# A Mamba block with an FP4 feed-forward layer on one core: where the C rows come from, and which VectorE operands lie in PSUM

## The reference

```
x = x + mamba(layernorm(x))
x = x + ffn(layernorm(x))
```

```
delta = softplus(dt_proj(dt_r) + dt_b)
s = s * exp(delta * A) + (delta * u) * B_t        # 128 channels x 16 states per head
y_t = sum over the 16 states of s * C_t
out = ((y + u * Dskip) * silu(z)) @ out_proj.T
```

## Time and profile before

| | |
|---|---|
| median of 3 runs | 6185.75 us (6184.68 to 6187.2) |
| span of the profiled execution | 6181.4 us |
| VectorE busy | 6057.9 us, 98% |
| GpSimd busy | 4848.8 us, 78% |
| TensorE busy | 4735.1 us, 77% |
| ScalarE busy | 4198.7 us, 68% |
| mean of the transfers | 10 GB/s |

### The profile page before, as it was taken

The page is one execution under the profiler, slowest core; times in us unless marked ns, Lnnn a source line. Parts: engine busy times, 40 slices in busy tenths (PEclk is TensorE's granted clock), DMA queues, the critical chain, the costliest instruction groups (busy, mean ns, idle before and its releaser), DMA issues.

```text
span 6181.4 us, 90775 instructions
## 1 busy us (share of the span) xinstructions
PE 4735.1 (77%) x14623; PEld 2333.3 (38%) x14892; DVE 6057.9 (98%) x8285; ACT 4198.7 (68%) x7312; POOL 4848.8 (78%) x4113
## 2 busy tenths in 40 slices
PE   4777777777777777777777777777777777777778
PEld 1233333333333333333333333333333333333334
DVE  7999999999999999999999999999999999999998
ACT  5766766676666667666676676666766766676663
POOL 6888777777787778777777787777777877787875
PEclk9999999999999999999999999999999999999999
DMA  1000000000000000000000000000000000000000
GB/s 43 5 8 9 9 9 11 9 9 9 12 8 9 9 12 9 9 9 11 9 9 9 12 9 9 9 11 9 9 9 11 9 9 9 12 9 9 9 6 13
DMA packets 59893, 62.59 MB, mean 10 GB/s; under 512 B 7014, under 2 KB 58342, under 8 KB 59110
## 3 DMA queue, kind: packets, MB, share of 16 engines
q1 hardware_dynamic: 57536, 53.68, 2.8%
q10 hardware_dynamic: 1702, 2.16, 0.1%
HBM read 39.04 MB, written 16.78 MB: 9 GB/s over the span
## 4 chain that ended last, share of the span: by engine, by line
DVE 45%; issue 26%; PE 21%; DVEq 4%; ACT 3%; POOL 1%; another core or an unknown queue 0%; DMA 0%; ACTq 0%; POOLq 0%
DVE state L824 14%; DVE db L814 8%; DVE acc L763 8%; PE ybank L892 6%; PE pbank L901 3%; DVEq L97 3%; PE db L879 3%; PE bank_b L947 2%; DVE v L647 2%; DVE spw L708 2%; PE bank_a L1017 2%; ACT decay L408 1%; DVE hh L758 1%; PE cbank L870 1%; PE bank_a L980 1%
## 5 line engine op out<-in xcount | busy, mean ns | idle before, releaser
L558 POOL TENSOR_TENSOR prod<-state,cs 128x512 f32<-128x512 f32 x2048 | 2777.2, 1356 | 1068.2 <-DVE state L824 1025.6
L395 ACT ACTIVATE cs<-cbank 128x512 f32<-128x512 f32 x2048 | 1217.0, 594 | 1184.3 <-PE cbank L870 993.4
L408 ACT ACTIVATE decay<-delta,aneg 128x512 f32<-128x512 f32 x2048 | 1455.1, 716 | 607.2 <-DVE state L824 599.4
L879 PE MATMUL db<-pieces,sel 128*128 128x512 bf16 x2031 | 807.5, 398 | 1345.7 <-DVE state L824 1309.8
L892 PE MATMUL ybank<-prod,ident 128*128 128x512 f32 x3072 | 1626.7, 619 | 2.7 <-POOL prod L562 2.6
L814 DVE TENSOR_TENSOR db<-db,du 128x512 f32<-128x512 f32 x2048 | 1394.4, 681 | 46.8 <-PE db L879 28.3
L824 DVE TENSOR_TENSOR_SCAN state<-decay,carry,db 128x512 f32<-128x512 f32 x1024 | 1286.7, 1257 | 0.0
L824 DVE TENSOR_TENSOR_SCAN state<-decay,db 128x512 f32<-128x512 f32 x1024 | 1229.3, 1200 | 0.0
L879 PEld LDWEIGHTS db<-pieces,sel 128*128 128x128 bf16 x2048 | 199.5, 97 | 2245.9 <-DVE state L824 2157.8
L562 POOL TENSOR_TENSOR prod<-prod 128x512 f32<-128x512 f32 x512 | 690.7, 1349 | 40.1
L870 PE MATMUL cbank<-pieces,sel 128*128 128x512 bf16 x1797 | 699.2, 389 | 14.9 <-ACT cs L395 13.9
(11 more groups left out here) (125 smaller groups left out, 7017.3 us busy)
## 6 DMA issues: line engine op xcount, KB each, us to landing
xin<-in_hidden SPq DMA_DIRECT2D x128, 128.0 KB, 2.0
xres<-in_hidden SPq DMA_DIRECT2D x128, 128.0 KB, 2.1
out_x<-ot SPq DMA_DIRECT2D x128, 128.0 KB, 1.9
win<-in_win_t SPq DMA_DIRECT2D x1, 1024.0 KB, 10.3
sel<-in_sel SPq DMA_DIRECT2D x1, 1024.0 KB, 14.9
state<-in_w_gate ACTq DMA_DIRECT2D x1, 704.0 KB
state<-in_w_up ACTq DMA_DIRECT2D x1, 704.0 KB
yg<-in_w_down ACTq DMA_DIRECT2D x1, 704.0 KB, 18.3
```

What stands on the lines that cost most here:

```text
L395: act.activation(cs[:, gc.k % RING, :], cbank[:, :], ACT.Copy).then_inc(c_copied, 1)
L408: act.activation(decay[:, g.k % RING, :], delta[:, gu % 2, :], ACT.Exp, scale=aneg[:, gu % HEADS, gn:gn + 1]).then_inc(decayed, 1)
L558: pool.tensor_tensor(prod[:, gn % RING, :], state[:, gn, :], cs[:, gn % RING, :], ALU.mult).then_inc(weighted, 1)
L879: pe.matmul(db[DB_BANK[g.k % TRIP]][:, :], sel[:, gn, :], pieces[:, gu % 2, :], start=True, stop=True).then_inc(b_spread, 1)
```

## The change

**C rows.** The matmul into `cbank`, the copy to `cs` and the upper half of the selection matrix go. ScalarE still makes `xdbl` in SBUF; SyncE now writes its 16 C rows to a DRAM buffer `c_rows` (32 KB for a unit), and reads them back two rows at a time, each pair as one transfer that repeats 4 KB on all 128 partitions (512 KB), into a ring of 4 buffers. A pair is asked for when the pair four places earlier has been weighted. GpSimd multiplies two states in one instruction of 1024 columns (`weigh`), and adds the two halves for the pairs 0, 2, 4 and 6 (`ADDED`), so the number of identity matmuls stays at 12 for a unit.

**Operands in PSUM.** The bank set free is `bank_c`. `z` is projected into it, while `x` stays in `pbank` and the convolution is carried out in place there (ScalarE makes tap 3, VectorE taps 0 to 2, with the shifted `x` from SBUF). `uu` reads `pbank`, the softplus correction reads `1 + e` from `bank_c`, and `yt` is written straight to `yg`.

**FP4 rounding.** ScalarE writes |x| times 2^22 to `bank_c`. VectorE reads the upper 16 bits of each word as BF16 and makes `x + max(that, ROUNDER)` and then the same with minus: two instructions for `v2`, and two for each half (352 columns) of `hh`.

Several slots move with it; `yt` goes from step 2 to step 3.

```diff
-PAIRED = (1, 6, 12, 14)
+PAIRS = NST // 2
+C_RING = 4
+P_RING = 4
+ADDED = (0, 2, 4, 6)
...
+            def spread_c(b, u, p):
+                slot = p % C_RING
+                free = held(sp, free_reg, u.val(PAIRS, p + 1 - C_RING))
+                if p == 0:
+                    rows_in = held(sp, rows_reg, u.val(16, 16))
+                    wait(sp, c_written, rows_in)
+                wait(sp, weighted, free)
+                rows = c_rows[u.mod(2), 2 * p:2 * p + 2, :].rearrange("n c -> (n c)")
+                sp.dma_start(cs[:, slot, :, :].rearrange("p n c -> p (n c)"),
+                             rows.unsqueeze(0).broadcast_to([P, 2 * CH])).then_inc(c_landed[slot], 16)
...
+                if n % 2:
+                    p = (n + 5) // 2
+                    w = u + p // PAIRS
+                    if w.within(UNITS):
+                        spread_c(b, w, p % PAIRS)
...
-                    act.activation(cs[:, gc.k % RING, :], cbank[:, :], ACT.Copy).then_inc(c_copied, 1)
+                if t := due("post", 48):
...
+                    act.activation(bank_c[:, 0:HALF], hv[t.mod(2)][:, 0:HALF], ACT.Abs, scale=POWER).then_inc(h_abs, 1)
...
+            def weigh(w, p):
+                c, r = p % C_RING, p % P_RING
+                wait(pool, scanned, w.val(NST, 2 * p + 2))
+                wait(pool, c_landed[c], w.val(16 * PAIRS // C_RING, 16 * (p // C_RING + 1)))
+                wait(pool, summed, w.val(PAIRS, p + 1 - P_RING))
+                pool.tensor_tensor(prod[:, r, :, :], state[:, 2 * p:2 * p + 2, :], cs[:, c, :, :],
+                                   ALU.mult).then_inc(weighted, 1)
...
-                dve.scalar_tensor_tensor(acc[:, :], xpad[:, h, k:k + CH], cw[:, h, k:k + 1], acc[:, :],
+                dve.scalar_tensor_tensor(pbank[:, :], x[:, k:k + CH], cw[:, h, k:k + 1], pbank[:, :],
...
+            def magnitude(n):
+                return bank_c[:, 0:n].bitcast(BF16).rearrange("p (n h) -> p n h", h=2)[:, :, 1]
+            def step_up(n, x):
+                return dve.scalar_tensor_tensor(hw[:, 0:n], magnitude(n), ROUNDER, x, ALU.max, ALU.add)
+            def step_down(n, x):
+                return dve.scalar_tensor_tensor(x, magnitude(n), ROUNDER, hw[:, 0:n], ALU.max, ALU.subtract)
...
-                    wait(pe, c_copied, g.val())
-                    pe.matmul(cbank[:, :], sel[:, NST + gn, :], pieces[:, gu % 2, :],
-                              start=True, stop=True).then_inc(c_spread, 1)
```

More of the change, by code:

```diff
@@ L102, in fresh, with held @@
     return b if isinstance(b, int) else eng.snap(b, min_val=1, max_val=BATCH - 2)
+def held(eng, reg, value):
+    if isinstance(value, int):
+        return value
+    eng.reg_mov(reg, value)
+    return reg
 def build(nc, hidden, win_t, conv_w, conv_b, xw, dtw, dt_b, a_log, dskip, wo_t, w_gate, w_up, w_down,
@@ L190, in build @@
         db = [bank(f"db{i}") for i in range(3)]
-        cbank = bank("cbank")
         ybank = bank("ybank")
         pbank = bank("pbank")
+        bank_c = bank("bank_c")
         bank_a = bank("bank_a")
@@ L361, in unit @@
-                t_o = Ix(b, j - 8, PER)
-                if t_o.within(TILES):
-                    wait(sp, o_done, t_o.val(plus=1))
-                    sp.dma_start(out_tiles[t_o.val()], ot[:, t_o.mod(2), :]).then_inc(ot_free[t_o.mod(2)], 16)
+                for n in range(NST):
+                    step(b, j, n)
             trips(sp, unit, constants)
@@ L462, in step @@
-                    act.activation(acc[:, :], xpad[:, h, 0:CH], ACT.Identity, bias=cb[:, h:h + 1],
-                                   scale=cw[:, h, 0:1]).then_inc(conv_op, 1)
+                    wait(act, x_mm, v.val(plus=1))
+                    wait(act, conv_op, v.val(TAPS))
+                    if v.mod(PER) < HEADS:
+                        act.activation(xearly[:, TAPS - 1:], pbank[:, :], ACT.Copy).then_inc(x_evac, 1)
+                        act.activation(halo[:, h, :], pbank[:, CH - TAPS + 1:], ACT.Copy).then_inc(x_evac, 1)
+                    else:
+                        wait(act, x_evac, v.val(2, -6))
+                        act.activation(xlate[:, 0:TAPS - 1], halo[:, h, :], ACT.Copy).then_inc(x_evac, 1)
+                        act.activation(xlate[:, TAPS - 1:], pbank[:, :], ACT.Copy).then_inc(x_evac, 1)
@@ L862, in step @@
                     spread_b(b, g)
-                for back in YSUM_BACK[n]:
-                    gy = Ix(b, j * NST + n - back, TRIP)
-                    if gy.within(STEPS) and gy.k % NST + 1 not in PAIRED:
-                        sum_up(b, gy)
+                if n % 2 == 0:
+                    w = u + (n - 4) // NST
+                    if w.within(UNITS):
+                        sum_up(w, (n - 4) // 2 % PAIRS)
                 side(b, u, due)
-                if g.within(STEPS):
-                    wait(pe, c_copied, g.val())
-                    pe.matmul(cbank[:, :], sel[:, NST + gn, :], pieces[:, gu % 2, :],
-                              start=True, stop=True).then_inc(c_spread, 1)
             def spread_b(b, g):
@@ L880, in spread_b, with sum_up @@
                           start=True, stop=True).then_inc(b_spread, 1)
-            def sum_up(b, g):
-                gu, gn = Ix(b, g.k // NST, PER), g.k % NST
-                first = gn == 0 or gn == 1 and 1 in PAIRED
-                if first:
-                    wait(pe, y_taken, gu.val())
-                if gn in PAIRED:
-                    wait(pe, paired, gu.val(len(PAIRED), PAIRED.index(gn) + 1))
-                else:
-                    wait(pe, weighted, g.val(plus=1))
-                pe.matmul(ybank[:, :], ident[:, :], prod[:, gn % RING, :],
-                          start=first, stop=(gn == NST - 1)).then_inc(summed, 2 if gn in PAIRED else 1)
+            def sum_up(w, p):
+                if p == 0:
+                    wait(pe, y_taken, w.val())
+                if p in ADDED:
+                    wait(pe, added, w.val(len(ADDED), ADDED.index(p) + 1))
+                else:
+                    wait(pe, weighted, w.val(PAIRS, p + 1))
+                for k in range(1 if p in ADDED else 2):
+                    last = pe.matmul(ybank[:, :], ident[:, :], prod[:, p % P_RING, k, :],
+                                     start=(p == 0), stop=(p == PAIRS - 1 and k == 1))
+                last.then_inc(summed, 1)
             def side(b, u, due):
```

237 lines of the change are left out of this document (126 added, 111 removed).

## The result

The changed kernel takes 5387.78 us (median of 4 runs, 5375.8 to 5392.47) against 6185.3 for the kernel before on the same chip: 0.8708 of it, with a 95% interval of 0.8695 to 0.872. The forecast was 5363, with 5250 to 5520 as its range. The profiled execution has a span of 5382.9 us, where the sum gave 5359.

A forecast was written before the change was run, and what follows sets the result against it. It took VectorE's queue as the bound: profiled 6181.4 - 927.1 (cheaper instructions) + 31 (lost overlap) + 74 (holds behind GpSimd) = 5359, with the median 4.35 higher, 5363 us; range 5250 to 5520.

The forecast's parts named there:

- VectorE is the bound, and busy time holds waits: VectorE's queue sets the time; its SBUF-only instructions stand still, counted as busy, until the GpSimd instruction ahead ends.
- Prices of the changed instructions: VectorE's taps, `uu`, correction and roundings priced by unblocked rows with a PSUM tensor, plus a dropped copy: -927.1 us.
- Why the rounding became cheap: VectorE's rounding with a PSUM tensor would not stand still behind GpSimd: `hh` -323.4 us, `v2` -174.1 us.
- Holds, +74: VectorE's small SBUF instructions held by GpSimd: scale of `hh` +51, `carry` copy +45, scale of `v2` -22 us.
- Waits, nothing: New waits in VectorE's queue for ScalarE and TensorE priced at nothing; `yt` tightest with 0.6 us left.
- The overlap, +31: Three VectorE instructions removed per unit take their 0.08 us overlap with them, so 31 us isn't won.
- C rows and the double product, nothing: C-row transfers, 4 MB a unit at 103 GB/s, priced at nothing; GpSimd keeps its arithmetic with 8 double products.
- GpSimd as the bound: Rival, chance 0.18: GpSimd keeps half its idle time and sets a 41.4 us unit; 102 us more, 5465.
- Half-word reads at half speed: Rival, chance 0.08: VectorE's reads of every second BF16 need a second cycle, 265 us more, 5628.
- PSUM doesn't free the taps: Rival, chance 0.03: taps, `uu` and correction on VectorE still stand behind GpSimd, keeping 419.6 us; 5783.
- PSUM dearer by 0.04 us: Rival, chance 0.04: each of 11 changed VectorE instructions a unit costs 0.04 us more, 56 us in all; 5420.
- Late C rows: Rival, chance 0.03: C-row transfers run one behind the other at 8.0 us each, starving GpSimd, then VectorE; 8280.

The follow-up runs named there:

- taps_sbuf: Changed kernel with the convolution and `uu` in an SBUF tensor `acc` again; 5877.64 us, ratio 0.9504.
- mag_sbuf: Changed kernel with |x| of the rounding in an SBUF tensor instead of PSUM, still two rounding instructions; 5423.82 us, ratio 0.877.
- round_sbuf: Changed kernel with the four rounding instructions of before, on SBUF tensors, without ScalarE's |x|; 6092.81 us, ratio 0.9853.
- half_bytes: Changed kernel with each C-row transfer bringing only the first row of its pair, 256 KB, odd states missing from y; 5382.26 us, ratio 0.8698.
- z_behind: Changed kernel with TensorE's z projection behind the down projection in steps 12 and 13; 5387.56 us, ratio 0.8711.

## Why the prediction was right, point by point

**VectorE is the bound, and busy time holds waits: shown.** VectorE is 96% busy after, and taps_sbuf changes on VectorE only where a tensor is, and is 490 us slower.

**Prices of the changed instructions: right, a little low.** Taps gave 243.5 us instead of 255.8 (744 ns for 712), `uu` 101.4 for 102.5, the correction 59.4 for 61.3, the rounding of `hh` 318.3 for 323.4, that of `v2` 170.3 for 174.1. With the copy of three columns that is -902.9 for the -927.1 of the sum.

**Why the rounding became cheap: half wrong.** The forecast put it, with the taps, under "a PSUM tensor doesn't stand still". The price was right, the reason was not: in mag_sbuf no tensor is in PSUM and the time rises by only 36 us. The other 669 us of round_sbuf come from the four instructions and where they start, above all the first, which GpSimd itself releases just before it takes up a product. The slot behind ScalarE's |x| moves that start behind the product. By the rows of round_sbuf some 166 us are the number and width of the instructions and some 531 the standstill; no run changed one of the two alone.

**Holds, +74: mis-sized, +8.** The scale of `hh` rose by 4 us and not 51, `carry` by 26 and not 45, the scale of `v2` fell by 22 as written. The count for `hh` had GpSimd end 0.4 us after VectorE's arrival, from 7.5 us of work. But I had taken the sum (1.35) and `v` (1.0) at their means of before, which held GpSimd's own waits behind VectorE, and the product as two of 1.29. The rows after give 2.36 + 1.27 + 0.62 + 1.27 + 1.27 = 6.8, less than the 7.1 that VectorE was counted at. When the standstill goes, GpSimd's instructions get shorter too.

**Waits, nothing: mis-sized, +73.** This is the step that failed. `yt` (now `yg`) was called the tightest, with 0.6 us in hand, and it waits 24.5 us for 5.8 before. In most units that margin holds: in the trace 25 of the 128 units wait more than 0.3 us, and 0.94 on average. `ot` waits 33.7 for 10.1; the forecast didn't name it. `db` waits 69.4 for 46.8, and 14 of these 23 us are the jumps of the loop. The rounding's new waits for |x| are 6.3 us. From jump to jump a unit takes 41.1 us instead of 47.5 and has TensorE 77% busy as before, but in a row of dependent steps, so I take it that its margins shrink with the unit. z_behind shows that putting one of them right hands the wait to the next.

**The overlap, +31: not seen.** Added up over its rows, VectorE's work overlaps by 640.1 us before and by 671.8 after, so 32 more, not 31 less. But the records of rows that the change doesn't touch are longer in this execution, by 56 us in sum. In half_bytes, with the same instructions and the same time, the rows add up to 57 us less and overlap by 618.1. So about 1% of a mean, and this term with it, lies within what one execution's records differ from another's.

The errors cancel in part: +24 by prices, -66 by holds, +73 by waits, -7 by overlap (-63) and longer records (+56), which is the +24 between 5359 and 5382.9. That the total is nearer than its terms is luck.

**C rows and the double product, nothing: right in the sum, not alone.** The transfers take 111 GB/s and 3.6 us, and but for some 6 us at the jumps of the loop (half_bytes) neither makes anyone wait. But by itself this part loses 453 us. In the forecast it was a small term with holds on it; the runs show that its cost depends on the rest of the change. Added up from the other side: +453 for the C rows, -490 for taps and `uu`, -705 for the rounding is -742, and the measured difference is -798. The 56 left are near the 61 of the correction, which was not run apart, and the sum holds only if the parts add. The bank of the C rows now takes `z`, which leaves `pbank` to the taps and `uu`, so the part that loses makes room for those that gain.

**The rivals.** None of the signs of being wrong came: the largest wait is `db`'s, 0.54 us a unit where 1 was the limit, and a double product takes 2.36 us. GpSimd as the bound: no, it waits 799 us ahead of its products. Half-word reads at half speed: no, 516 ns for 352 columns. PSUM doesn't free the taps: no, 744 ns in the middle of a product. PSUM dearer by 0.04 us: for the taps alone, 744 for 712, and not for `uu` and the correction (680, 687). Late C rows: no. The fixed cost of the Trainium skill ("VectorE: DVE Perf Modes", on the TRN2 errata; by the prediction's estimate 65 ns more for a PSUM source) does not show: the same instruction of 352 columns takes 504 ns with `bank_c` and 501 with `mag` in SBUF, and the second one of `v2` 401 and 399.

## What to carry to other kernels

When VectorE is full, look in its timeline for instructions that are longer than their columns, and ask what GpSimd is doing at their start. There are three ways out, and they are not the same: put one tensor into PSUM, so that it never matters; start the instruction behind the GpSimd one and not under it; or make the GpSimd instruction shorter. A longer GpSimd instruction is a good trade only once the VectorE work beside it is out of its way: the same step from two short products to one long lost 323 us in one kernel and won 27 in the other.

Price the waits anew when the unit gets shorter by a seventh. Margins of half a microsecond are gone then, and a wait taken away at one place comes back at the next.
